# Requantising the hidden row on VectorE instead of ScalarE, with scratch columns of their own, in the FFN half of an AdaLN block

## The reference

```python
def bitlinear(x, w, b):
    xq = act_quant(rmsnorm(x))      # per token: round(x*127/max|x|), clipped, and back
    wq = weight_quant(w)            # ternary: -1, 0, 1 times a scale
    return jnp.einsum('bsd,fd->bsf', xq, wq) + b
...
h = _layernorm(x, axis=-1) * (1 + cb) + sb
h = bitlinear(h, w1, b1)            # 1024 -> 4096
h = jax.nn.gelu(h, approximate=False)
x = x + gb * bitlinear(h, w2, b2)   # 4096 -> 1024
```

## Time and profile before

| what | value |
|---|---|
| time, median of 2 runs | 6471.98 us (6471.77 to 6472.18) |
| the profiled execution | 6473.35 us |
| span of its slowest core (core 3) | 6471.4 us |
| spans of the 8 cores | 6451.2 to 6471.4 us |
| mean granted TensorE clock of the cores | 0.680 to 0.684 |
| busy PE, DVE, ACT over the span | 2668.6, 3591.6, 2329.1 us |
| attention half | up to about 4040 us |
| weights made ternary | to about 4533 us |
| 32 units of the FFN | about 4537 to 6471 us |

### The profile page before, as it was taken

One profiled execution on the slowest core, in us unless ns is written; L12 is line 12 of the kernel. 1 busy time (PEld: TensorE's weight loads), 2 busy tenths in 40 slices (PEclk: granted clock), 3 DMA queues, 4 the chain that ended last, 5 costly groups with the idle time before them and its releaser, 6 DMA issues.

```text
span 6471.4 us, 48362 instructions; the slowest of 8 cores (6451.2 to 6471.4 us)
## 1 busy us (share of the span) xinstructions
PE 2668.6 (41%) x12096; PEld 1391.2 (21%) x12096; DVE 3591.6 (56%) x8990; ACT 2329.1 (36%) x4155; POOL 26.2 (0%) x53
## 2 busy tenths in 40 slices
PE   5612333233323323332333232000666666666666
PEld 5511222122112212221221121000222222222222
DVE  0127656755675576567566754888544444444442
ACT  0005334433543453344335433000444444444444
POOL 0000000000000000000000000000000000000000
PEclk9995665566556656665665565555778887887888
DMA  2130000000000000000000003300000000000000
GB/s 99 59 77 1 14 14 13 1 14 14 1 14 14 13 1 14 14 13 1 14 14 5 9 7 65 59 0 0 14 14 20 20 14 20 20 20 14 20 17 10
DMA packets 31708, 123.08 MB, mean 19 GB/s; under 512 B 4756, under 2 KB 6565, under 8 KB 29382
## 3 DMA queue, kind: packets, MB, share of 16 engines
q1 hardware_dynamic: 24486, 98.95, 4.2%
q0 software_dynamic: 6944, 21.05, 2.0%
HBM read 106.95 MB, written 34.08 MB: 22 GB/s over the span
## 4 chain that ended last, share of the span: by engine, by line
DVE 38%; PE 21%; ACT 14%; DVEq 9%; DMA 7%; issue 6%; ACTq 4%; SPq 1%; POOLq 0%
PE psY L41 13%; DVEq L324 6%; DVE are_bf L1012 5%; DVE zz L875 5%; PE psZ L41 4%; DVE aim_bf L1018 4%; ACTq L324 3%; ACT wstage L1490 3%; PE psMC L41 3%; ACT h_act L1494 2%; DVE nbuf L979 2%; ACT sin_bf L988 2%; DMA x_sb<-xmid 2%; DVE aim_bf L1003 2%; DMA x_sb<-x 1%
## 5 line engine op out<-in xcount | busy, mean ns | idle before, releaser
L41 PE MATMUL psZ<-pw_sb,sel_sb 32*128 32x256 f32 x256 | 146.6, 686 | 1321.9 <-DVEq L324 852.1
L41 PE MATMUL psY<-w1q,q1f 128*128 128x512 bf16 x2048 | 546.5, 415 | 298.2 <-ACTq L324 298.0
L41 PE MATMUL psY<-w2q,q2f 128*128 128x512 bf16 x2048 | 515.3, 413 | 20.0 <-ACTq L324 20.0
L41 PE MATMUL psZ<-hbf,win 128*128 128x256 bf16 (+1 forms) x2176 | 310.2, 304 | 243.3 <-ACTq L324 241.5
L41 PE MATMUL psY<-are_bf,bd_sb 128*128 128x256 bf16 x512 | 130.8, 410 | 656.5 <-ACTq L324 646.5
L1012 DVE TENSOR_TENSOR_SCAN are_bf<-are_bf,ncar_re 128x256 bf16<-128x256 bf16 x512 | 374.7, 732 | 16.4 <-issue 1.4
L1018 DVE TENSOR_TENSOR_SCAN aim_bf<-aim_bf,ncar_im 128x256 bf16<-128x256 bf16 x512 | 371.6, 726 | 0.0
L41 PEld LDWEIGHTS psZ<-pw_sb,sel_sb 32*128 32x128 f32 x256 | 66.1, 309 | 1380.3 <-issue 1377.3
L1447 ACT ACTIVATE h_act<-psY,al 128x512 bf16<-128x512 f32 x256 | 176.0, 687 | 463.9 <-PE psY L41 452.7
L875 DVE SCALAR_TENSOR_TENSOR zz<-z,wcv_sb,zz 128x256 f32<-128x256 f32 (+1 forms) x816 | 326.7, 478 | 5.9
L1467 DVE BATCH_NORM_STATS2 bnst<-h_act 128x6 f32<-128x512 bf16 x256 | 177.7, 694 | 249.4 <-ACTq L324 218.2
(11 more groups left out here) (217 smaller groups left out, 5716.3 us busy)
## 6 DMA issues: line engine op xcount, KB each, us to landing
wmstg<-wmod SPq DMA_DIRECT2D x8, 3072.0 KB, 11.0
x_sb<-x SPq DMA_DIRECT2D x32, 512.0 KB, 5.9
xmid<-xo_sb SPq DMA_DIRECT2D x32, 512.0 KB, 3.1
x_sb<-xmid SPq DMA_DIRECT2D x32, 512.0 KB, 4.0
out<-xo_sb SPq DMA_DIRECT2D x32, 512.0 KB, 2.9
w1q<-w1T POOLq DMA_DIRECT2D x8, 1024.0 KB, 24.8
w2q<-w2T POOLq DMA_DIRECT2D x32, 256.0 KB, 5.6
win<-in_proj_w POOLq DMA_DIRECT2D x8, 520.0 KB, 6.1
```

The lines of the kernel that those rows point to most:

```text
L41: r = _a(*args, **kw)
```

## The change

Three things, all in the 32 units:

1. `s_q2h` moves from ACT to DVE. Its two activations become two `tensor_scalar` instructions on the same 128x512 pieces, the first from bf16 to f32, the second back. It stands at the same place in the list of stages.
2. The small numbers of a unit leave the shared tile: `fa` and `fb` for the front, `da` and `db` for the back, four of each, with names of their own. `s_q2h` now reads `da`; `s_cs2b` reads `da` and `bnst2` and writes `db`; `s_q1` reads `fa`, and `s_cs1b` reads `c2` and `fa` and writes `fb`. The arithmetic on them is the same.
3. `qrsqrt` takes its columns as arguments. It issues the same instructions.

The core of the diff (renamings of the same kind left out):

```diff
+            fap = [sb(f"fa_{i}", (128, 4), F32, SB) for i in range(4)]
+            fbp = [sb(f"fb_{i}", (128, 8), F32, SB) for i in range(4)]
+            dap = [sb(f"da_{i}", (128, 4), F32, SB) for i in range(4)]
+            dbp = [sb(f"db_{i}", (128, 8), F32, SB) for i in range(4)]
...
-            def qrsqrt(e, c2, dst, src):
+            def qrsqrt(e, dst, src, tmp, hx):
...
                 b.stage("vector", s_h2,
                         reads=(f"x{tpar}{s}", cn, "cb1B", "sbB"),
-                        writes=("h2", "bnst", cn))
+                        writes=("h2", "bnst", cn, fan))
...
-                b.stage("scalar", s_q1, reads=("h2", cn),
+                b.stage("scalar", s_q1, reads=("h2", fan),
                         writes=("q1", "h2"))
...
-                b.stage("vector", s_cs1b, reads=(cn, "smallc"),
-                        writes=(cn, f"al1_{u8}", f"iac1{up}"))
+                b.stage("vector", s_cs1b, reads=(cn, fan, "smallc"),
+                        writes=(fbn, f"al1_{u8}", f"iac1{up}"))
...
-                b.stage("vector", s_cs2a, reads=("amx",), writes=(cn,))
+                b.stage("vector", s_cs2a, reads=("amx",), writes=(dan,))
 
                 for hh in range(8):
-                    def s_q2h(e, c2=c2, hh=hh):
+                    def s_q2h(e, da=da, hh=hh):
                         hs = hh * 512
-                        e.activation(out=wstage[:], in_=h_act[:, hs:hs + 512],
-                                     func=AF.Copy, scale=col(c2, 11),
-                                     bias=MAGIC)
+                        e.tensor_scalar(out=wstage[:], in0=h_act[:, hs:hs + 512],
+                                        scalar1=col(da, 2), scalar2=MAGIC,
+                                        op0=ALU.mult, op1=ALU.add)
                         e.drain()
-                        e.activation(out=h_act[:, hs:hs + 512], in_=wstage[:],
-                                     func=AF.Copy, bias=-MAGIC)
-                    b.stage("scalar", s_q2h, reads=(f"ha{hh}", cn),
+                        e.tensor_scalar(out=h_act[:, hs:hs + 512], in0=wstage[:],
+                                        scalar1=MAGIC, scalar2=None,
+                                        op0=ALU.subtract)
+                    b.stage("vector", s_q2h, reads=(f"ha{hh}", dan),
                             writes=(f"ha{hh}", "wstage"))
...
-                b.stage("vector", s_cs2b, reads=(cn, "smallc", "bnst2"),
-                        writes=(cn, f"al2_{u8}", f"iac2{up}"))
+                b.stage("vector", s_cs2b, reads=(dan, "smallc", "bnst2"),
+                        writes=(dbn, f"al2_{u8}", f"iac2{up}"))
```

More of the change, by code:

```diff
@@ L1285, in build_nc @@
             I32 = mybir.dt.int32
-            def qrsqrt(e, c2, dst, src):
-                d_i = col(c2, dst).bitcast(I32)
-                e.tensor_scalar(out=d_i, in0=col(c2, src).bitcast(I32),
+            def qrsqrt(e, dst, src, tmp, hx):
+                d_i = dst.bitcast(I32)
+                e.tensor_scalar(out=d_i, in0=src.bitcast(I32),
                                 scalar1=1, scalar2=None,
                                 op0=ALU.logical_shift_right)
-                e.tensor_scalar(out=col(c2, 1), in0=col(c2, src),
+                e.tensor_scalar(out=hx, in0=src,
                                 scalar1=-0.5, scalar2=None, op0=ALU.mult)
@@ L1298, in qrsqrt @@
                 for _ in range(2):
-                    e.tensor_tensor(out=col(c2, 0), in0=col(c2, dst),
-                                    in1=col(c2, dst), op=ALU.mult)
+                    e.tensor_tensor(out=tmp, in0=dst, in1=dst, op=ALU.mult)
                     e.drain()
-                    e.tensor_scalar(out=col(c2, 0), in0=col(c2, 0),
-                                    scalar1=col(c2, 1), scalar2=1.5,
+                    e.tensor_scalar(out=tmp, in0=tmp,
+                                    scalar1=hx, scalar2=1.5,
                                     op0=ALU.mult, op1=ALU.add)
                     e.drain()
-                    e.tensor_tensor(out=col(c2, dst), in0=col(c2, dst),
-                                    in1=col(c2, 0), op=ALU.mult)
+                    e.tensor_tensor(out=dst, in0=dst, in1=tmp, op=ALU.mult)
                     e.drain()
@@ L1317, in p2_front @@
                 cn = f"c2_{up}"
+                fa, fan = fap[up], f"fa{up}"
+                fb, fbn = fbp[up], f"fb{up}"
                 ia_row = iarp[up]
@@ L1335, in s_ln2 @@
                     e.drain()
-                    qrsqrt(e, c2, 5, 4)
+                    qrsqrt(e, col(c2, 5), col(c2, 4), col(c2, 0), col(c2, 1))
                 b.stage("vector", s_ln2, reads=(f"x{tpar}{s}",),
@@ L1352, in s_h2 @@
                     e.bn_stats(out=bnst[:, 6:12], in_=h2_sb[:, 512:1024])
-                    e.reduce_max(out=col(c2, 7), in_=h2_sb[:], axis=AX,
+                    e.reduce_max(out=col(fa, 0), in_=h2_sb[:], axis=AX,
                                  apply_absolute_value=True)
@@ L1366, in s_h2 @@
                     e.drain()
-                    e.tensor_scalar(out=col(c2, 10), in0=col(c2, 7),
+                    e.tensor_scalar(out=col(fa, 1), in0=col(fa, 0),
                                     scalar1=1e-6, scalar2=None, op0=ALU.max)
                     e.drain()
-                    e.reciprocal(out=col(c2, 10), in_=col(c2, 10))
+                    e.reciprocal(out=col(fa, 1), in_=col(fa, 1))
                     e.drain()
-                    e.tensor_scalar(out=col(c2, 11), in0=col(c2, 10),
+                    e.tensor_scalar(out=col(fa, 2), in0=col(fa, 1),
                                     scalar1=127.0, scalar2=None, op0=ALU.mult)
@@ L1375, in p2_front, with s_q1 @@
                         reads=(f"x{tpar}{s}", cn, "cb1B", "sbB"),
-                        writes=("h2", "bnst", cn))
-                def s_q1(e, c2=c2):
+                        writes=("h2", "bnst", cn, fan))
+                def s_q1(e, fa=fa):
                     e.activation(out=h2_sb[:], in_=h2_sb[:], func=AF.Copy,
-                                 scale=col(c2, 11), bias=MAGIC)
+                                 scale=col(fa, 2), bias=MAGIC)
                     e.drain()
@@ L1383, in s_q1, with s_cs1b @@
                                  bias=-MAGIC)
-                b.stage("scalar", s_q1, reads=("h2", cn),
+                b.stage("scalar", s_q1, reads=("h2", fan),
                         writes=("q1", "h2"))
[L1387 to L1390, removed]
+                def s_cs1b(e, c2=c2, fa=fa, fb=fb):
+                    qrsqrt(e, col(fb, 2), col(c2, 6), col(fb, 0), col(fb, 1))
+                    e.tensor_tensor(out=col(fb, 3), in0=col(fa, 0),
+                                    in1=col(fb, 2), op=ALU.mult)
                     e.drain()
-                    e.tensor_scalar(out=al1[u8][:, 0:1], in0=col(c2, 9),
+                    e.tensor_scalar(out=al1[u8][:, 0:1], in0=col(fb, 3),
                                     scalar1=col(smallc, 0),
@@ L1396, in s_cs1b @@
                     e.drain()
-                    e.reciprocal(out=col(c2, 14), in_=al1[u8][:, 0:1])
+                    e.reciprocal(out=col(fb, 4), in_=al1[u8][:, 0:1])
                     e.drain()
-                    e.tensor_copy(out=iacol1[up][:], in_=col(c2, 14))
-                b.stage("vector", s_cs1b, reads=(cn, "smallc"),
-                        writes=(cn, f"al1_{u8}", f"iac1{up}"))
+                    e.tensor_copy(out=iacol1[up][:], in_=col(fb, 4))
+                b.stage("vector", s_cs1b, reads=(cn, fan, "smallc"),
+                        writes=(fbn, f"al1_{u8}", f"iac1{up}"))
                 def s_iat(e, up=up):
@@ L1461, in p2_back @@
                 cn = f"c2_{up}"
+                da, dan = dap[up], f"da{up}"
+                db, dbn = dbp[up], f"db{up}"
                 ia_row = iarp[up]
@@ L1473, in p2_back, with s_cs2a @@
                             writes=("bnst2", "amx"))
-                def s_cs2a(e, c2=c2):
-                    e.reduce_max(out=col(c2, 7), in_=amx[:, 0:8], axis=AX)
+                def s_cs2a(e, da=da):
+                    e.reduce_max(out=col(da, 0), in_=amx[:, 0:8], axis=AX)
                     e.drain()
-                    e.tensor_scalar(out=col(c2, 10), in0=col(c2, 7),
+                    e.tensor_scalar(out=col(da, 1), in0=col(da, 0),
                                     scalar1=1e-6, scalar2=None, op0=ALU.max)
@@ L1480, in s_cs2a @@
                     e.drain()
-                    e.reciprocal(out=col(c2, 10), in_=col(c2, 10))
+                    e.reciprocal(out=col(da, 1), in_=col(da, 1))
                     e.drain()
-                    e.tensor_scalar(out=col(c2, 11), in0=col(c2, 10),
+                    e.tensor_scalar(out=col(da, 2), in0=col(da, 1),
                                     scalar1=127.0, scalar2=None, op0=ALU.mult)
-                b.stage("vector", s_cs2a, reads=("amx",), writes=(cn,))
+                b.stage("vector", s_cs2a, reads=("amx",), writes=(dan,))
```

(30 more changed lines are left out.)

## The result

The changed kernel takes 6536.94 us (median of 7 runs, 6535.95 to 6538.90) against 6476.11 us for the kernel before, timed beside it (6 runs): a ratio of 1.0096, 95% interval 1.0083 to 1.0108, so 0.96% slower. That is +61 us, with 6499 us forecast and a range of 6440 to 6595.

A forecast was written before the change was run, and what follows sets the result against it. No engine is full; a chain of waits bounds the 32 FFN units. 6473.35 - 158.7 (rounding) + 217.3 (order) - 31 (clock) = 6501 us profiled, so 6499 us forecast (+0.4%), range 6440 to 6595.

The forecast's parts named there:

- Term 1: Between `s_cs2a` and `s_cs2b`: rounding on DVE starts `s_cs2b` 4.96 us earlier per unit, -158.7 us over 32 units.
- Term 2: DVE order: the planner puts `s_h2` between statistics 5 and 6, on the chain; 7.76 us in 28 units, +217.3 us.
- Term 3: PE before and in half 0: shorter idle time keeps the clock up more; 1.0 us a unit, -31 us.
- no clock gain: Rival: forecast's order, PE clock as now, 6531 us; included in the 0.70 for the forecast's order.
- `s_h2` off the chain: Rival on DVE: `s_h2` stays behind `s_cs2b`; 6313 us without clock gain, middle 6288; chance 0.15.
- slow pace of 692 ns: Rival: DVE rounding passes run at 692 ns; +122 us, 6620 us, chance 0.05.
- `s_cs1b` ahead: Rival: `s_cs1b(u+3)` also lands ahead of `s_q2h`; +96 us, 6594; chance 0.10, shared with similar delays.
- What was hidden: Parts priced at nothing: w1 0 and w1 1 shifting around PE's idle time, `s_q1(u+3)` on ACT beside half 0.

The follow-up runs named there:

- e1: Changed kernel with one dependence more, so the planner puts `s_h2` behind `s_cs2b`; 6310.07 us, ratio 0.9736 to the kernel before.
- e5: Changed kernel plus 20 unused 128x256 matmuls per unit on PE before `s_ia2t`; 6533.63 us, ratio 1.0071 to the kernel before.
- e9: e5 plus 6 more 128x256 matmuls behind the transposes of group 0; 6484.90 us, ratio 1.0005 to the kernel before.
- e2: e1 with `s_ln2` placed behind `s_cs2b` as well; 6202.63 us, ratio 0.9569 to the kernel before.
- e6: e2 with the inverse scale's transpose given its own PSUM place and put behind half 0; 5960.81 us, ratio 0.9190 to the kernel before.

## Why the prediction was right, and where not

- **Term 1, the rounding.** 4.94 us a unit measured in the unit shown, 4.96 forecast. The rows of the weight stages held to the nanosecond: 486 and 427 ns. By the formula that the prediction takes from the Trainium skill (VectorE: DVE Perf Modes, the TRN2 errata) it would be 327 ns, an estimate; none of the 512 instructions is that short. The same section says of its formula that it under-predicts and puts the measured fixed term near 150 cycles instead of 58, which the prediction left out; with it the estimate is 423 ns, and the trace has 427.
- **Term 2, the order.** The order is the one worked out, in 28 units as forecast, and the slot of `s_h2` costs 7.77 us, 7.76 forecast. e1 shows it as the cause by taking it away. Terms 1 and 2 together were +58.6 us; the measured +61 has an interval of about 54 to 70.
- **Term 3, the clock,** was the step that failed: -31 us forecast, nothing came. Half 0 takes 8.84 us in the changed kernel and 8.85 before, each the mean of 32 units (the prediction's 8.90 was over 25 of them). Idle PE time ahead of the small transpose did shrink about as worked out, to 3.7 us in the unit shown and 4.2 as the mean (3.9 forecast, 8.0 as the mean before), but the clock falls in it all the same. Windows of 1 us, the changed kernel (PEclk third from the end):

```profile
5214.00:5215.00 1.00, 0.00 (x0) 0.00 (x0) 0.71 (x5) 0.00 (x0) 0.00 (x0) 1.00 0.00 0
...
5216.00:5217.00 1.00, 0.00 (x0) 0.00 (x0) 0.69 (x4) 0.00 (x0) 0.00 (x0) 0.92 0.00 0
5217.00:5218.00 1.00, 0.48 (x4) 0.25 (x5) 0.73 (x5) 0.38 (x2) 0.00 (x0) 0.50 0.00 0
...
5254.00:5255.00 1.00, 0.00 (x0) 0.00 (x0) 0.83 (x2) 1.00 (x7) 0.00 (x0) 0.69 0.00 0
```

  PE ended w1 1 at 5213.4 and the clock fell before 5217, some 3.5 us later. After the w1 slice that ended at 5252.7 it fell before 5255, within 2.4 us, and w1 0, which the prediction had at full clock, took 3.57 us there. I took a little over half of a gain whose condition, "near the 4.5 us after which it fell here", came from one fall, and that length did not hold for these. And e5 shows that even with the idle time filled the thin work between the transposes lets it fall; the gain exists (59 us in e9, with matmuls added) but was not to be had from this change. Without term 3 the forecast would have been 6530, the rival "no clock gain" 6531, within 6 us of the result.
- **The rivals.** `s_h2` off the chain: 6310 measured in e1, 6313 forecast for it without clock gain. The price was right, but this agreement is in part luck: by the ratio e1 is 0.9736 of 6472, 6301 us, and the 12 us between them are about the 13 of the shorter half 0 in e1, which that forecast left out. The order was not this one. The slow pace of 692 ns and `s_cs1b` ahead did not happen.
- **What was hidden** stayed hidden: `s_q1(u+3)` on ACT, w1 0 and w1 1 on PE.
- **Not settled:** why the mean of half 0 differs between e1 (8.41) and the changed kernel (8.84) with the same idle time ahead (4.3 and 4.2 us as means). From unit to unit it changes between some 8.4 and 9.5 us in the changed kernel, while in e1 most units take 8.0 to 8.8; no run isolates the reason.

## What to carry to other kernels

When a stage moves to another engine, work out the whole new order before pricing the move: the engine that is set free lets stages run ahead, and a planner that takes what can start first will lay them in front of the chain. One name in a dependence list decided 233 us here; the faster rounding is worth 158 (4.94 us in 32 units). And look at which result each wait on the chain truly serves: the small transpose was needed half a matmul stage later than it stood, and taking it off the chain was worth 246 us by the ratios (e2 to e6), 42 of them by the full clock in half 0, more than the faster engine.

## What the runs showed of the hardware

- A 128x512 `tensor_scalar` takes 486 ns with its scalar in a column, whether it reads bf16 or f32 (both write f32), and 427 ns with a constant, whether it writes bf16 or f32 (both read f32); the changed kernel and the earlier trace rows.
- PE's granted clock fell about 3.5 us after its last matmul at one place of the changed kernel, within 2.4 us at another, and 4.5 us after it at one of the kernel before. In one unit of e5 it rose before 5215 and fell again before 5222 with no idle time over 1.5 us since, where PE had 20 short matmuls and then only groups of eight 128-column transposes between waits. With six short matmuls more in one of these gaps (e9), half 0 ran at full clock in the unit shown, 7.07 us, and took 7.45 as the mean. At the level of 1.2 GHz a group of eight transposes took 1.01 us, at 2.4 GHz 0.61.
